# Two mixture-of-experts layers: every token through every expert, against tokens grouped by expert in DRAM

## The reference

```python
logits = xf @ Wg.T + bg                      # 4096 tokens x 8 experts
probs = softmax(logits); tp, ti = top_k(probs, 2)
tp = tp / (sum(tp) + 1e-8)
w = sum(one_hot(ti, 8) * tp[..., None], axis=1)
h = gelu(einsum('td,efd->tef', xf, W1) + b1)
y = einsum('tef,edf->ted', h, W2) + b2
out = einsum('ted,te->td', y, w)
x = x + gb * (h_in + out)
```

## Time and profile before

| | us |
|---|---|
| median of 3 runs (2423.88 to 2432.16) | 2430.76 |
| the profiled execution | 2425.25 |
| its span | 2423.5 |
| mean granted clock of TensorE, share of full | 0.906 |
| TensorE busy | 2001.8 (83%) |
| VectorE busy | 1824.0 (75%) |
| ScalarE busy | 1393.0 (57%) |
| GpSimd busy | 527.5 (22%) |

### The profile page before, as it was taken

How to read it: one execution, slowest core, us unless ns; L and a number is a source line. 1 busy time by engine, 2 the same in 40 slices (tenths; PEclk the granted TensorE clock), 3 DMA queues, 4 the chain that set the end, 5 groups by cost and what they waited for, 6 DMA issues and landing times. The chain is left out here.

```text
span 2423.5 us, 36959 instructions
## 1 busy us (share of the span) xinstructions
PE 2001.8 (83%) x12584; PEld 1173.2 (48%) x12584; DVE 1824.0 (75%) x3749; ACT 1393.0 (57%) x3262; POOL 527.5 (22%) x516
## 2 busy tenths in 40 slices
PE   7898998989737999999459999999999842458887
PEld 3477786768536777767211222222222232435554
DVE  5554554545577988989789999999999267389987
ACT  3265665656535555555314888888888841244444
POOL 3022222222371211212500000000000040443322
PEclk9899999999858999999767999999999966679999
DMA  3011111111010000000030101010100000010001
GB/s 119 9 34 27 34 34 27 34 27 34 18 49 28 1 0 0 0 0 0 31 106 15 30 15 29 16 29 16 29 16 15 1 1 2 4 40 0 0 0 35
DMA packets 48315, 54.94 MB, mean 23 GB/s; under 512 B 9976, under 2 KB 35728, under 8 KB 48016
## 3 DMA queue, kind: packets, MB, share of 16 engines
q1 hardware_dynamic: 47556, 51.99, 7.7%
q10 hardware_dynamic: 588, 0.81, 0.1%
HBM read 27.88 MB, written 8.78 MB: 15 GB/s over the span
## 5 line engine op out<-in xcount | busy, mean ns | idle before, releaser
L1621 ACT ACTIVATE probs<-s_ps 128x512 f32<-128x512 f32 x1024 | 534.0, 603 | 140.8 <-PE s_ps L1552 140.6
L1639 DVE TENSOR_REDUCE q_max<-s_ps 128x1 f32<-128x1024 f32 x512 | 599.2, 1219 | 11.8 <-PE s_ps L1531 5.5
L1531 PE MATMUL s_ps<-k_stack,q_stack 64*128 64x512 bf16 x1024 | 358.0, 404 | 21.4 <-PEq L86 10.8
L1158 DVE TENSOR_TENSOR moe_hid_lo<-moe_hid,moe_hid_hi 128x512 fp32r<-128x512 f32 x384 | 330.9, 862 | 13.1
L1552 PE MATMUL s_ps<-q_stack,k_stack 64*128 64x512 bf16 x1024 | 314.9, 384 | 21.0 <-ACT probs L1621 14.5
L1566 PE MATMUL o_ps<-probs,v_aug 128*32 128x512 f32 x2048 | 273.6, 606 | 0.7 <-ACT probs L1621 0.7
L1126 POOL TENSOR_TENSOR nat<-nat,moe_ym 128x512 f32 x112 | 157.6, 1407 | 533.1 <-DVE moe_ym L1139 533.1
L1107 ACT ACTIVATE moe_hid<-moe_hps,moe_b 128x512 f32<-128x512 f32 x256 | 175.9, 688 | 154.0 <-PE moe_hps L1069 86.2
L1552 PEld LDWEIGHTS s_ps<-q_stack,k_stack 64*128 64x128 bf16 x1024 | 78.2, 94 | 336.4 <-ACT probs L1621 285.2
L734 ACT ACTIVATE probs<-s_biased,s_min 128x128 f32<-128x128 f32 x512 | 199.6, 395 | 44.8 <-DVE s_min L772 44.8
L799 POOL TENSOR_TENSOR probs<-probs,p_rsum 128x512 f32<-128x512 f32 x128 | 133.1, 1040 | 374.9 <-DVE p_rsum L778 374.9
(11 more groups left out here) (289 smaller groups left out, 3444.4 us busy)
## 6 DMA issues: line engine op xcount, KB each, us to landing
v_shift<-v_tiles SPq DMA_DIRECT2D x32, 256.0 KB, 3.1
v_shift<-v_tiles SPq DMA_DIRECT2D x32, 224.0 KB, 3.6
qk_parts_dram<-qk_parts SPq DMA_DIRECT2D x16, 384.0 KB, 2.4
q_stack<-qk_parts_dram SPq DMA_DIRECT2D x180, 32.0 KB
k_stack<-qk_parts_dram SPq DMA_DIRECT2D x180, 32.0 KB
x<-in_L_attn_x SPq DMA_DIRECT2D x4, 512.0 KB, 7.2
rt_raw<-in_L_ffn_W1T SPq DMA_DIRECT2D x8, 256.0 KB, 3.3
rt_raw<-in_L_ffn_W2T SPq DMA_DIRECT2D x8, 256.0 KB, 3.1
```

Of the source, the lines that this page charges most:

```text
L1158: v.tensor_tensor(hid[1][:, s % 2, f, :], hf[:, n % 3, :], hid[0][:, s % 2, f, :].bitcast(F32), ALU.subtract).then_inc(hid_lo, 1)
L1531: mm = nc.tensor.matmul(s1[u % 2][:, c * CH:(c + 1) * CH], qs[head_rows(m), quad % 4, j, qt * P:(qt + 1) * P], ks[head_rows(m), quad % 4, ...
L1621: nc.scalar.activation(pr[:, k % 2, HEADS[pos], :], bank_of("exp", n)[:], ACT.Exp).then_inc(sm["exp"], 1)
L1639: v.tensor_reduce(mx[:, quad % 2, col:col + 1], s1[u % 2][:], AX.X, ALU.max).then_inc(sm["maxed"], 1)
```

## The change

Both expert layers are replaced. Each token goes only through its two experts.

- **Rows in DRAM.** `K.moe_rows` has 34,560 rows of 128 floats (17.7 MB), 4096 for each expert and 256 between. In `rms_stage`, behind the memsets of GpSimd, all of it is set to zero by six DMAs from GpSimd; SyncE waits for them after the window attention.
- **Routing per sequence, inside the norm stage.** The chain of VectorE is now done for 8 tiles at a time (`shift_logits`, `choose`). `place` counts, with two matmuls (a triangular matrix and one of ones), how many tokens before this one chose each expert; this gives two row numbers (slots) per token. `tabulate` makes a table of 39 blocks of 256 rows: for each its expert and its first row. Blocks past the end have expert 7 and rows that hold zeros or nothing needed.
- **Scatter.** Per tile and choice one indirect DMA of GpSimd writes the normalised tile (before the affine step) to its rows: 64 in a layer.
- **Blocks.** `block_stage`: for each of 39 blocks SyncE reads the expert and the row from the table, loads the rows and the expert's matrices (one DMA of 4624 or 2048 bytes a partition), TensorE turns the rows over, VectorE does the affine step, TensorE multiplies in plain float32, ScalarE does the gelu, TensorE the second matrix, VectorE copies the result (and adds the bias), SyncE stores it into the same rows. The residual (`nat` times gate, into `x`) is done by VectorE beside blocks 0 to 7.
- **Gather.** 64 indirect DMAs of GpSimd read the two result rows of each token; VectorE weighs and sums them, multiplies with the gate, adds to `x`.

`routing_stage`, `expert_stage` and `Experts` are gone. The matrices and biases of an expert lie side by side in one input array.

```diff
@@ window_attention_stage, fill(pool)
+            nc.gpsimd.memset(zero[:], 0.0).then_inc(filled, 1)
+            pool.wait_ge(filled, 4)
+            rows = K.moe_rows.rearrange("(p r) d -> p (r d)", p=P)
+            for n in range(ROWS // P // ZR // 9):
+                part = rows[:, 9 * n * ZR * D:9 * (n + 1) * ZR * D].rearrange("p (k z) -> p k z", k=9)
+                pool.dma_start(part, bc(zero[:], 1, 9)).then_inc(cleared, 16)
...
+                sp.wait_ge(cleared, 16 * (ROWS // P // ZR // 9))
@@ double_norm_stage (last_norm_stage likewise)
-                for b in range(B + 3):
+                for b in range(B + 3 + 2 * (M is not None)):
+                    if M and 4 <= b < B + 4:
+                        M.shift_logits(dve, b - 4)
...
+                    if M and 4 <= b < B + 4:
+                        M.choose(dve, b - 4)
+                    if M and b >= 5:
+                        M.place(dve, b - 5)
+                if M:
+                    M.tabulate(dve)
...
+                if M:
+                    for b in range(B):
+                        M.scatter(pool, N2, b)
+                    M.wait_scattered(pool)
@@ class RoutedExperts
+    def place(self, dve, b):
+        v, step = self.nc.vector, self.step
+        dve.wait_ge(self.prefixed, b + 1)
+        total = self.cp[b % 2][:, 1, 0:TPB * E].rearrange("p (t e) -> p t e", e=E)
+        for t in range(TPB):
+            k = b * TPB + t
+            step(dve, v.tensor_tensor(self.cum[:, k + 1, :], total[:, t, :], self.cum[:, k, :], ALU.add))
...
+    def scatter(self, pool, N, b):
+        pool.wait_ge(self.placed, b + 1)
+        N.wait_normalised(pool, (b + 1) * TPB)
         for t in range(b * TPB, (b + 1) * TPB):
+            for c in range(2):
+                self.nc.gpsimd.indirect_dma_start(
+                    self.K.moe_rows, bass.IndirectOffsetOnAxis(ap=self.slot[:, c, t:t + 1], axis=0), N.hat[:, t, :], None
+                ).then_inc(self.scattered, 16)
@@ block_stage: XB, WBUF, YB = 4, 4, 3; H = 2; BR = 256; NBK = 39
+            @block.sync
+            def _(sp):
+                rows = {}
+                for j in range(NBK + 2):
+                    if j < NBK:
+                        e = nc.sync.value_load(M.table[0:1, 0, j:j + 1], min_val=0, max_val=E - 1)
+                        rows[j] = nc.sync.value_load(M.table[0:1, 1, j:j + 1], min_val=0, max_val=ROWS - BR)
+                        if j >= XB:
+                            sp.wait_ge(turned, j - XB + 1)
+                        sp.dma_start(xi[:, j % XB], K.moe_rows[bass.ds(rows[j], BR), :].rearrange("(p a) d -> p a d", a=H)
+                                     ).then_inc(x_in[j % XB], 16)
+                        if j >= WBUF:
+                            sp.wait_ge(y_out, j - WBUF + 1)
+                        sp.dma_start(wb[:, j % WBUF, :], M.blocks[bass.ds(e, 1)].rearrange("e p w -> p (e w)")
+                                     ).then_inc(w_in[j % WBUF], 16)
+                    if j >= 2:
+                        k = j - 2
+                        sp.wait_ge(y_out, k + 1)
+                        sp.dma_start(K.moe_rows[bass.ds(rows.pop(k), BR), :].rearrange("(p a) d -> p a d", a=H),
+                                     ys[:, k % YB]).then_inc(stored[k % YB], 16)
+            @block.tensor
+            def _(pe):
+                def turn(j):
+                    pe.wait_ge(x_in[j % XB], 16 * (j // XB + 1))
...
+                turn(0)
+                for j in range(NBK + 1):
+                    if j + 1 < NBK:
+                        turn(j + 1)
+                    if j < NBK:
+                        hidden(j)
+                    if j >= 1:
+                        out_rows(j - 1)
...
+                tokens_out(0)
+                for j in range(NBK + 1):
+                    if j + 1 < NBK:
+                        tokens_out(j + 1)
+                    if j >= 1:
+                        rows_out(j - 1)
+                    if 2 <= j < NCH + 2:
+                        residual(j - 2)
@@ gather_stage
+                for t in range(NT):
+                    for c in range(2):
+                        nc.gpsimd.indirect_dma_start(
+                            yg[:, t, c, :], None, K.moe_rows, bass.IndirectOffsetOnAxis(ap=M.slot[:, c, t:t + 1], axis=0)
+                        ).then_inc(got[t // CPT], 16)
```

More of the change, by code:

```diff
@@ L1009, in logits @@
-    def logits(self, nc, K, pe, N, b):
-        pe.wait_ge(N.turn_read, 2 * b + 2)
-        pe.wait_ge(self.router_loaded, 16 * (2 + (self.bias_in is not None)))
-        for t in range(b * TPB, (b + 1) * TPB):
-            nc.tensor.matmul(self.lp[:, t, :], K.hT[:, t * P:(t + 1) * P], self.wg[:], start=True, stop=True)
-def expert_stage(nc, K, name, M, gelu, layer, out=None):
+            loads.append((self.bg[:], self.bias_in.partition_broadcast(P)))
+        for dst, src in loads:
+            sp.dma_start(dst, src).then_inc(self.router_loaded, 16)
@@ new lines, in load_router, with wait_router, logits @@
+        sp.wait_ge(self.router_loaded, 16 * len(loads))
+    def wait_router(self, eng):
+        eng.wait_ge(self.router_loaded, 16 * (4 + (self.bias_in is not None)))
+    def logits(self, pe, N, b):
+        pe.wait_ge(N.turn_read, 2 * b + 2)
+        self.wait_router(pe)
+        if b >= 2:
+            pe.wait_ge(self.shifted, b - 1)
+        for t in range(TPB):
+            k = b * TPB + t
+            m = self.nc.tensor.matmul(self.lp[b % 2][:, t, :], self.K.hT[:, k * P:(k + 1) * P], self.wg[:],
+                                      start=True, stop=True)
+        m.then_inc(self.logit_mm, 1)
@@ new lines, in tabulate @@
+    def tabulate(self, dve):
+        v, step = self.nc.vector, self.step
+        base, marks = self.steps[:, 0:E], self.steps[:, E:E + STEPS_OF]
+        number = self.steps[:, E + STEPS_OF:]
+        blocks, first, upto = (self.nb[:, i, :] for i in range(3))
+        passed, spent = self.le[:, 0], self.le[:, 1]
+        expert, row, rest = (self.tf[:, i, :] for i in range(3))
+        step(dve, v.tensor_tensor(first, self.cum[:, NT, :], base, ALU.subtract))
+        step(dve, v.tensor_tensor(self.over[:], bc(first, 2, STEPS_OF), bc(marks, 1, E), ALU.is_gt))
+        step(dve, v.tensor_reduce(blocks, self.over[:], AX.X, ALU.add))
+        g4 = self.gt[:, 0, :].rearrange("p (a b) -> p a b", a=E)
+        step(dve, v.tensor_tensor(g4, bc(blocks, 1, E), self.low[:].rearrange("p (a b) -> p a b", a=E), ALU.mult))
+        step(dve, v.tensor_reduce(first, g4, AX.X, ALU.add))
+        step(dve, v.tensor_tensor(upto, first, blocks, ALU.add))
+        step(dve, v.tensor_tensor(passed, bc(upto, 1, NBK), bc(number, 2, E), ALU.is_le))
+        step(dve, v.tensor_tensor(spent, passed, bc(blocks, 1, NBK), ALU.mult))
+        v.tensor_reduce(expert, passed, AX.X, ALU.add)
+        step(dve, v.tensor_reduce(rest, spent, AX.X, ALU.add))
+        step(dve, v.tensor_tensor(rest, number, rest, ALU.subtract))
+        step(dve, v.tensor_scalar(rest, rest, float(BR), None, ALU.mult))
+        step(dve, v.scalar_tensor_tensor(out=row, in0=expert, scalar=float(SPAN), in1=rest, op0=ALU.mult,
+                                         op1=ALU.add))
+        step(dve, v.tensor_scalar(expert, expert, float(E - 1), None, ALU.min))
+        v.tensor_copy(self.table[:], self.tf[:, 0:2, :])
```

620 lines of the change are left out of this document (278 added, 342 removed).

## The result

The changed kernel takes 2738.8 us (median of 4 runs, 2738.4 to 2743.2). Beside it the kernel before took 2429.6 (2423.9 to 2432.2): a ratio of 1.128, 95% interval 1.126 to 1.130, some 309 us more. The profiled execution took 2738.61 and its span is 2736.4, 312.9 more than before's span.

What follows compares the result with a forecast made beforehand. It took TensorE as the first expert layer's bound and VectorE's splitting of hidden values as the second's. First layer +79, second +183.5 and zeroing +8 made +270: 2695 us, range 2420 to 2980.

Steps and rivals of the forecast that it cites:

- The order of SyncE's list: Expert blocks: the next block's rows are requested only after an earlier store, leaving TensorE idle 4 to 6 us per block.
- The chain, 4.7 us: Each block round: matmul end, copy, hand-overs, store issue, two register loads and rows in, beside which TensorE idles, 4.7 us.
- The work on TensorE, 3.7 and 1.96 us at full clock: TensorE's transposes and matmuls per block: 3.7 us in the first expert layer, 1.96 in the second.
- The clock, and the blocks' totals: Expert blocks: granted clock 0.75 and 0.55, rounds 9.6 and 8.3 us, totals 388 and 336 us.
- rival 3: Expert blocks: TensorE stays at its lower level throughout, rounds 12.1 and 8.6 us, 2807 us in all; chance 0.15.
- The indirect DMAs: Scatters and gathers: GpSimd issues 64 of each per layer one by one, 1.05 us each, barely hidden.
- Rival 2: Scatters, gathers and blocks: indirect DMAs at 0.43 us and near-free register loads, 2358 to 2420 us; chance 0.12.
- The ends of the stages: Norm stages: 2 us from the last scatter to the stage's end.
- The zeroing: Six DMAs on GpSimd at the kernel's start: 0 to 35 us more, taken as 8.
- first of my two cases: Zeroing at the kernel's start: if GpSimd only issues the DMAs, it costs 0.
- Rival 4: Scatters and gathers: GpSimd is held up by VectorE's SBUF work, up to 126 us, 2821 us in all; chance 0.12.
- Rival 1: Expert blocks: rows arrive in time, so TensorE's work and the weights' transfers set the round, 2213 us; chance 0.06.

Runs made afterwards that it cites:

- the repair: The changed kernel with table values read a block ahead and stores one block later: 2314.5 us; with the stores also issued by GpSimd: 2307.2 us.

## Why the prediction was right

The sign and the mechanism were right. The forecast was 270 us more; it came to 313 in the profiled executions that it was summed against, and to 309 by the medians. The miss, 43 us of 2739, is a sum of terms of both signs, and that the blocks' totals came so near is in part luck, as shown below.

**The order of SyncE's list** (right). TensorE waits for the DMA of x in gaps of 4.3 us once a block, within the 4 to 6 forecast; they are 36 a layer, not 39, as the rows of the first three blocks are asked for before any store. That the list and nothing else makes them is shown by the run with the later stores: nothing changed but that, and 396 us went.

**The chain, 4.7 us** (near in sum, wrong in two parts of opposite sign). From the copy's start to the transposes are 4.24 us; with the last matmul's overhang (0.17) and the hand-over to VectorE (0.05) 4.46. Two register loads: I took 0.43 each; store's issue to rows' issue is 1.69, and 0.55 in the run that has no loads between them, so 0.57 each. My nearest row was the wrong relative: a load from memory is not an issue. The Trainium skill's figure of at least about 600 ns (DMA: Bandwidth & Descriptors, Latency and other measured facts) is a little above what this trace shows. Rows to TensorE: I took 2.65, with 0.45 for the queue behind the store; it is 2.06, so the store ahead is not in the way.

**The work on TensorE, 3.7 and 1.96 us at full clock** (right): 3.74 measured where nothing else binds.

**The clock, and the blocks' totals** (near in sum, wrong in parts that cancel). The granted clock over the blocks was 0.74 for 0.75 and 0.62 for 0.55. But the sum used the number as the clock at which the columns run, and the mean takes in the gaps. TensorE's work in a round was 5.9 us, not 4.9, and 4.0, not 3.6: the second is the lower level nearly throughout, twice 1.96. With gaps of 4.3 instead of 4.7 a round came to 10.2 for 9.6 and 8.3 for 8.3. The second term mis-sized is the number of rounds: 36 have the chain, not 40, and the time around them was 24 and 17.5 us where the sum has 42 and 37 (four rounds and 4 us). In the first layer the two errors cancel (391 us for 388); in the second the 20 us between 316 and 336 are the rounds counted too many, not the clock. So rival 3 (chance 0.15) did occur in the second layer, at 8.3 us for its 8.6, and not in the first, at 10.2 for its 12.1. The run with idle matmuls shows what was paid in both: 138 us.

**The indirect DMAs** (1.05 forecast, 1.27 measured). This is the largest term mis-sized: 256 x 0.22 = 56 us. The middle between an issue and a small operation was near the busy time, 0.95; the 0.30 between two of them was not in the sum. Half the scatters confirm the price, 1.27 each and 1.33 with the shorter stage ends. Rival 2 (0.43) is excluded by this.

**The ends of the stages.** 2 us forecast behind the last scatter, 8.7 and 8.3 measured: +13. With these, scatters and gathers explain 69 of the 74 us that the four stages took beyond the sum: 149.5 for 126, 121.2 for 97, 88.6 for 75, 90.4 for 78. The start of the scatters was right in the first layer (712.5 for 711) and 4 us late in the second (32 us behind the norms' start for 28).

**The second layer before.** I counted it from 2096 as 327.5; its first work is at 2091.4, 332.1. That is 4.6 of the miss, in the other direction.

**The zeroing** (8 forecast, nothing measured: the norms start 1.3 us earlier than before, within the spread of 651.4 to 653.7 among the runs without a second zeroing). The bytes went at 380 to 400 GB/s, not 285, and were down at 99.9 us; the barrier opened at 101.5 by TensorE's and VectorE's own work (100.6). So the 0 is true by a margin of under 2 us. The first of my two cases, "only issues", lacks a part: GpSimd goes on, but the barrier behind it waits for the landing, as the second pass issued by GpSimd shows and the one issued by ScalarE confirms.

**Rival 4** (GpSimd held up by VectorE). No. The gathers run beside 26 us of VectorE's work in SBUF and have a median of 0.945 and a maximum of 1.15; the scatters, beside 32 to 37 us, 0.96. The float32 product of the earlier trace rows slowed an operation on data fivefold; none of these operations did that to an indirect DMA: gathers that lie wholly beside VectorE's weighing and summing take the same 0.94 as those beside nothing. The rule of the Trainium skill cited for it (SBUF — State Buffer, SBUF: two separate sides) is not settled by this: it speaks of operations that hold the port, and no run here shows whether these do.

**Rival 1** (rows there in time). Not for the kernel as changed, but it is what the repair gives: my 2213 for it stands beside 2314 and 2307. (Its 160 us for the first layer's blocks are 8 more than 40 rounds of 3.7 and 4, and are given no reason.) What it lacked is mainly the indirect DMAs and stage ends (some 69 us, as above), and in the second layer rounds of 2.9 or 2.46 instead of 2.

## What to carry to other kernels

Buffers don't make a pipeline; the order of the issuing engine's list does. Write out for one round what stands behind each wait: here a load for the next block stood behind the store of a block that TensorE had only just finished, and moving that store by one block was worth 396 of 2739 us and turned a loss of 13% into a gain of 3%. Where tokens are moved by indirect DMAs of 128 rows, price them one by one (here 256 x 1.27 = 325 us, more than the 221 of all the blocks' TensorE work at full clock), and before a barrier ask what GpSimd has outstanding. And do not take the mean granted clock of a stretch with gaps for the clock of the columns: look at how long equal matmuls take in it.

## What the runs showed of the hardware

- An all-engine barrier opened 1.6 us after the last landing of DMAs issued by GpSimd (150.6 and 149.0), though nobody waited for them, and did not wait for those issued by ScalarE.
- GpSimd issued six DMAs of 2880 KB in 6.3 us; ScalarE's queue took two such DMAs in 0.44 and 0.70 us and then 6.4 to 7.5 for each while earlier ones drained.
- Writes of zeros from SBUF to DRAM ran at 380 to 400 GB/s.
- An indirect DMA of 128 rows of 512 B keeps GpSimd 0.95 us, and the next starts 1.26 to 1.27 after it, in both directions, with or without VectorE beside it.
- Behind the last scatter the barrier opened 8.7 and 8.3 us later (6.5 and 5.7 with half as many), though the bytes were moved within 1 us. Why is open.
- Two register loads from a table in SBUF took SyncE 1.14 us together.
- Work of no use in TensorE's gaps raised its granted clock from 0.74 and 0.62 to 1.00 and 0.99, and saved 138 us.
- TensorE's granted clock can be 0.50 while it works and 1.00 in the gap behind it (2412.8 to 2416.9 and 2418.5 to 2420.0), so a mean of 0.62 went with a first matrix whose columns all ran at the lower level: 634 ns a row, 379 with the gaps filled.
